# Three work lists of a memory layer reordered: ScalarE's copy, TensorE's turn and mixing, VectorE's addition

## The reference, cut to what matters

```
q = (xn @ w_q.T)                                # two halves of each of 8 heads
sim = einsum('pbnhd,hkpd->pbnhk', q, keys)      # 32 keys a half and head
s, i = top_k(sim, 8)                            # the 8 best of each half
scores, pk = top_k(sx[..., :, None] + sy[..., None, :], 8)   # the 8 best pairs of 64
o = gelu(inputs . key_in[idx]) * softmax(scores)
out = sum over the chosen pairs of o * key_out[idx]
```

## Time and profile before

| | |
|---|---|
| median of 3 runs | 2702.46 us (2686.27 to 2704.49) |
| the profiled execution's own time | 2697.36 us |
| its span, first to last instruction | 2695.5 us |
| mean granted TensorE clock | 0.944 |
| busy: PE, DVE, ACT, POOL | 88%, 75%, 72%, 37% of the span |
| memory stage, first key scores to last mixing | 584.7 to 1376.7 us |

### The profile page before, as it was taken

The page is one execution under the profiler, slowest core; times in us unless marked ns, Lnnn a source line. Parts: engine busy times, 40 slices in busy tenths (PEclk is TensorE's granted clock), DMA queues, the critical chain, the costliest instruction groups (busy, mean ns, idle before and its releaser), DMA issues. The chain is left out here.

```text
span 2695.5 us, 94302 instructions
## 1 busy us (share of the span) xinstructions
PE 2359.0 (88%) x34124; PEld 1784.0 (66%) x34124; DVE 2029.3 (75%) x5391; ACT 1946.6 (72%) x3656; POOL 988.8 (37%) x1267
## 2 busy tenths in 40 slices
PE   2999935967888888888879999899899999999999
PEld 1666623635666666666656767566678788888887
DVE  6788888767788888888747777678766777777776
ACT  1888853866688888888747777777667777777776
POOL 1455510447688777777723333233200000000000
PEclk9999975967799999999989999899899999999999
DMA  5000000000000000000020000011011111111111
GB/s 178 1 0 0 0 16 0 1 3 8 7 6 6 5 6 6 6 6 5 7 64 1 0 0 0 22 42 42 21 52 47 48 51 55 51 55 51 56 54 47
DMA packets 66029, 69.09 MB, mean 26 GB/s; under 512 B 8720, under 2 KB 44304, under 8 KB 65808
## 3 DMA queue, kind: packets, MB, share of 16 engines
q1 hardware_dynamic: 65936, 67.85, 8.3%
HBM read 59.17 MB, written 4.46 MB: 24 GB/s over the span
## 5 line engine op out<-in xcount | busy, mean ns | idle before, releaser
L567 POOL TENSOR_TENSOR work<-work,consts_sb 128x1024 f32<-128x1024 f32 x128 | 246.1, 1923 | 368.5 <-ACT work L741 346.5
L1280 PEld LDWEIGHTS ps<-work 32*32 32x32 f32 x16384 | 242.7, 145 | 117.8 <-issue 117.8
L1280 PE MATMUL ps<-work 32*32 32x32 f32 x16384 | 250.2, 225 | 64.0 <-DVE work L1799 46.4
L2002 DVE TENSOR_TENSOR h_low<-consts_sb,h_up 128x1024 fp32r<-128x1024 f32 x128 | 156.8, 1225 | 116.2 <-ACT h_up L983 116.2
L1606 DVE TENSOR_REDUCE work<-ps 128x8 f32<-128x512 f32 x256 | 169.9, 686 | 87.5 <-PE ps L1094 81.7
L1368 PE MATMUL ps<-a_low,w_up 128*128 128x512 f32 x512 | 205.9, 402 | 0.0
L1390 PE MATMUL ps<-h_low,d_up 128*128 128x512 f32 x512 | 200.1, 391 | 2.2 <-DVE h_low L2002 2.2
L1370 PE MATMUL ps<-a_up,w_low 128*128 128x512 f32 x512 | 201.2, 393 | 0.0
L1369 PE MATMUL ps<-a_up,w_up 128*128 128x512 f32 x512 | 200.8, 392 | 0.0
L1392 PE MATMUL ps<-h_up,d_low 128*128 128x512 f32 x512 | 199.5, 390 | 0.0
L1391 PE MATMUL ps<-h_up,d_up 128*128 128x512 f32 x512 | 199.3, 389 | 0.0
(11 more groups left out here) (298 smaller groups left out, 6365.0 us busy)
## 6 DMA issues: line engine op xcount, KB each, us to landing
gates_spread<-gate_rows SPq DMA_DIRECT2D x128, 256.0 KB, 3.1
ctxT_all<-in_ctxT SPq DMA_DIRECT2D x1, 4096.0 KB, 13.0
work<-big SPq DMA_DIRECT2D x64, 64.0 KB, 1.9
work<-in_ctx SPq DMA_DIRECT2D x64, 64.0 KB, 1.8
work<-in_ctxT SPq DMA_DIRECT2D x64, 64.0 KB, 1.8
out<-x_all SPq DMA_DIRECT2D x16, 256.0 KB, 3.5
big<-in_up SPq DMA_DIRECT2D x1, 2048.0 KB, 9.0
consts_sb<-in_consts SPq DMA_DIRECT2D x1, 936.0 KB
```

Source lines behind the costliest of these rows:

```text
L567: pool.tensor_tensor(KX[:, u].rearrange("p b (h k) -> p b h k", h=PER_SET), KC[:, u].unsqueeze(2).to_broadcast([P, 2, PER_SET, SEQ]), own_ ...
L1280: ins = pe.matmul(psW[rows, n // 16, :, n % 16], XT[rows, T.u, :, n], YT[rows, T.u, :, n], start=True, stop=True)
L2002: dve.tensor_tensor(h_low[:, n], hid[n], h_up[:, n].bitcast(F32), ALU.subtract).then_inc(h_split, 1)
```

## The change

Three lists of segments are changed, and nothing inside a segment.

- ScalarE: `copy_gated` goes from lag 6, behind the one-hot rows, to lag 7, second in the step behind `normed`. It works one step later on the same tile. The largest lag grows from 6 to 7, so that ten steps are written out ahead of the loop, where it was eight.
- TensorE: the order `mixed`, `key_scores`, `turn_gated`, `hidden`, `spread_heads` becomes `key_scores`, `hidden`, `mixed`, `spread_heads`, `turn_gated`. The lags stay.
- VectorE: `add_memory` gets lag 7 for 6, at the same place in the list, behind `turn_back`.

```diff
-            staggered(nc, act, NT, [(0, normed), (2, exps_before_gelu), (5, hidden), (2, exps_after_gelu), (2, best_one_hot), (6, copy_gated), (3, above_floor),
+            staggered(nc, act, NT, [(0, normed), (7, copy_gated), (2, exps_before_gelu), (5, hidden), (2, exps_after_gelu), (2, best_one_hot), (3, above_floor),
                                     (3, scaled_one_hots)])
...
-            staggered(nc, pe, NT, [(7, mixed), (0, key_scores), (6, turn_gated), (4, hidden), (4, spread_heads)])
+            staggered(nc, pe, NT, [(0, key_scores), (4, hidden), (7, mixed), (4, spread_heads), (6, turn_gated)])
...
-                                    (3, turn_sides), (4, turn_back), (6, add_memory), (2, pair_shares), (0, best_less)])
+                                    (3, turn_sides), (4, turn_back), (7, add_memory), (2, pair_shares), (0, best_less)])
```

## The result

The changed kernel takes 3027.28 us in the median of 4 runs (3026.49 to 3029.39) against 2702.81 us before, the median of 4 runs too; the ratio is 1.122, 95% interval 1.119 to 1.126. Forecast were 3010 us in a range of 2900 to 3085.

What follows compares the result with a forecast made beforehand. A ring in the memory stage set 11.59 us a step; the new rings average 15.4, 17.0 with TensorE's low clock. 56 steps +303, less 17, +7, end +20: +313, from 2697 to 3010 us, range 2900 to 3085.

Steps and rivals of the forecast that it cites:

- the first: TensorE's turn waits for spreading, back transpose and addition of the same step: 1.13 + 0.25 us with TensorE doing nothing.
- Rings at full clock: Memory-stage loop, from copy to copy: 16.3 us with exponentials behind the GELU, 14.45 us in the other steps.
- The clock: TensorE's low level in the loop: turn +0.9 us a step, hidden product +0.8 in the mean, less 0.1 leeway.
- The rival that kept the clock up: TensorE stays at full clock in the new steps: 56 x 3.8 us more, 2915 us in all; chance 0.15.
- Mean step 17.0: Memory-stage loop with TensorE's low clock counted: 17.0 us a step for 11.59, +303 us over 56 steps.
- The steps written out ahead of the loop: Some six steps already at 14.5 us: 17 us given back, +7 for TensorE's issue waits on the new ring.
- The -17: Some six of steps 8 to 63 took 14.5 us already and not 11.59, which gives back 17 us.
- The end: Last eight steps of the stage: two full ones, then a ring of some 12.5 us for 11, +20 us.
- GpSimd's branch: Long steps, exponentials' end to `turn_back`: 9.8 us over GpSimd's step and gating, against 8.4 on the other branch.
- the spreading's branch: Long steps, candidates over VectorE's top pairs, top keys and difference to TensorE's spreading: 8.4 us to `turn_back`, hidden by 1.4.
- the rival for "faster": Turn and copy leave the old ring, the copy never waits: steps some 10.6 us, 2640 us; chance 0.02.
- the rival for "no change": Ring without the wait for addition and difference: 11.6 us a step in the mean, 2700 us; chance 0.02.

Runs made afterwards that it cites:

- the gating early: The changed kernel with GpSimd's `gated` right behind the candidates instead of last: 3031.9 us, a step of 17.05 us.
- the last run: The changed kernel with GpSimd's `gated` right behind the candidates and VectorE's `pair_floors` (L1824) moved behind the addition: 3016.8 us, ratio 1.121.

## Why the prediction was right

The step that carries it is the first: a turn that waits for an addition in the same step, behind a back transpose, behind the spreading, closes a ring through all four engines. The brackets of the changed kernel name its members, ScalarE's part alone is faster than before and TensorE's part alone far slower, and the addition taken out from behind the back transpose gives 113 us back.

Term by term:
- Rings at full clock, 16.3 and 14.45: measured 16.40 and 14.26 in the kernel with its idle time filled. With the low clock the terms give 17.2 and 16.85; measured from turn to turn are 17.31 and 16.82.
- The clock, 17.0 - 15.4 = +1.6 a step, 90 us in the sum: 17.04 - 15.32 = 1.72 from the two kernels, and 86 us by their ratios. Slow were the turn in every step (1.94 us, forecast 1.9) and the hidden product in every second (3.61, forecast 3.5), and the mixing behind it was fast again (1.95). For that last point the prediction leans on rows 6, which show nothing behind the hidden product: that it came true is luck as far as the rows go. The rule on idle gaps in the Trainium skill, "TensorE: Matmul & The Clock Gate", section "HAM oscillation — how this bites in real kernels", would by the prediction's reading have kept the clock up. This trace does not agree with that: no idle piece of TensorE's between 800 and 1400 us is over 2.99 us, and the granted clock was 0.74. The rival that kept the clock up lay at 2915 us.
- Mean step 17.0: measured 17.04. Steps 14 to 64 give 50 x 5.45 = 272.7 us of the 329.9 that the span grew.
- The steps written out ahead of the loop, from the eighth key scores to the fourteenth: 107.9 us for 83.2, +24.7; the prediction's terms give 6 x 5.41 - 17 + 7 = 22.5. The -17 took 14.5 us for each of these steps before, from one of them; their mean is 13.9 (83.2 / 6), so that it should have been -14.
- The end, from the last key scores to the end of the last mixing: 101.0 us for 66.5, so +34.5, forecast +20. This is the term that was mis-sized, and most of the 17 us between forecast and result. I had put the ring of the last steps at 12.5 us with TensorE at full clock. The last full ones in the trace run slow:

```profile
1672.71 1.94 PE L1288 MATMUL ps<-consts_sb,work 128*128 128x128 f32 x8 [1.63 <-DVE x_all L1860]
1676.68 3.78 PE L1268 MATMUL ps<-work 128*128 128x512 f32 x4 [2.03 <-ACT work L914]
1680.26 2.50 PE L1294 MATMUL ps<-w 128*128 128x128 f32 x16
1682.69 2.81 PE L1280 MATMUL ps<-work 32*32 32x32 f32 x180
1686.66 1.33 PE L1280 MATMUL ps<-work 32*32 32x32 f32 x76 [1.16 <-issue]
1689.61 1.94 PE L1288 MATMUL ps<-consts_sb,work 128*128 128x128 f32 x8 [1.63 <-DVE x_all L1860]
```

From turn to turn that is 16.9 us (1672.71 to 1689.61): turn and hidden product slow, the mixing 2.50 for 2.05, and 1.16 us of waiting for issue in the spreading, which is on the ring here. I had counted the low clock in the loop and the waits for issue in the steps ahead of it, and neither at the end.

Two statements were right in kind and off in detail. GpSimd's branch was to lead VectorE's by 1.4 us; it leads by 0.6. VectorE's work from the start of its top pairs (L1817) to the end of the side transposes (L1850) is 8.12 us (1013.26 to 1021.38) and has `chosen` and the side transposes in it, where I took the spreading's branch for the second longest. And the rival for "faster" was close to a real mechanism, but it belongs to a part of the change: the copy a step later pays when the turn stays early, 10.89 us a step against the 10.6 named there. The terms of the rival for "no change" add up to 11.7 us and not to its 11.6, which moves nothing else.

## What to carry to other kernels

In a stage of several in-order lists, moving a piece of work a step later pays if what releases it is then done early enough that it never waits, as with the copy in ScalarE's part alone; write out for each moved wait which list position its releaser has, and add up the loop that it closes, before counting what leaves the old loop. A change that is several reorders at once can hold a gain and a loss: here one of three lists alone gave 1.3%, and the three together lost 12%. And where the new loop leaves TensorE idle longer than the old one did, price its work on the loop at both levels of the clock, ends of the stage included, and take the prices from rows of the same kernel.

## What the runs showed that I had not expected

TensorE filled with work that nobody needs made the kernel 86 us faster, as its turn went from 1.94 to 1.09 us and its hidden product in the short steps from 3.61 to 1.98. The granted clock was 0.98 with idle pieces of up to 1.5 us left in every step, against 0.74 with pieces of 0.5 to 3.0.

VectorE's L1824, 128x8 numbers, takes 0.15 us or anything up to 1.7. In the kernel before, 54 of its 64 executions were over 0.2 us, and every one of these began while a GpSimd instruction ran and ended within 0.06 us of that instruction's end; in the changed kernel 58 of 58, with the gating early 60 of 60. In the last run, which moved L1824 to where GpSimd mostly rests, 62 of 64 began with no GpSimd instruction running, and all 62 took under 0.2 us. The groups by line in the changed kernel and in the one with the gating early:

```profile
L1824 DVE TENSOR_SCALAR work<-work 128x8 f32<-128x8 f32 x64 | 27.8, 435 | 0.2
```
```profile
L1824 DVE TENSOR_SCALAR work<-work 128x8 f32<-128x8 f32 x64 | 80.0, 1249 | 0.2
```

So it ends with what GpSimd has begun, and is shown as busy meanwhile: 27.8 us in all became 80.0 when the gating, GpSimd's longest instruction, and the second one-hot behind it came to lie beside it. There are exceptions: in the kernel before, two short executions began with over 0.25 us of GpSimd's L639 to go. What holds it up no trace names. The Trainium skill, "SBUF — State Buffer", section "SBUF: two separate sides", has VectorE and GpSimd share a pair of ports by an exclusive lock for the whole instruction, if VectorE's runs in a 2-port mode or has two SBUF inputs. The trace agrees with such a lock in when the long executions end (54 of 54); whether L1824, with its one input, runs in that mode no run here shows.
